# A two-layer graph kernel: its preparation is cut into pieces beside the first node stage, and the target scatters wait for each other in twos

## The chip, the cores and the metric

The kernel runs on one core of a Trainium2 chip. The metric is the device time of one execution in microseconds (us). Engines are called by their names: TensorE (PE in the profile), VectorE (DVE), ScalarE (ACT), GpSimd (POOL) and SyncE (SP).

## What is computed

Two graph layers over 50,000 nodes of 256 float32 features. The edges are 25,000 random ones and a loop at every node, 75,000 in all, sorted by target. Cut to what matters:

```python
h = relu(layernorm(x))
# layer 1: x = x + gcn(batchnorm_mlp(h))
h = h @ w1.T + b1
h = relu((h - mean) * rsqrt(var + eps) * gamma + beta)   # mean, var over all nodes
xw = (h @ w2.T + b2) @ w_gcn.T
deg = segment_sum(ones, dst);  dinv = rsqrt(max(deg, 1))
x = x + segment_sum(xw[src] * (dinv[src] * dinv[dst])[:, None], dst) + b_gcn
# layer 2: edge softmax with 8 heads
h = relu(layernorm(x))
q, k, v = (h @ Wq + bq) * s, h @ Wk + bk, h @ Wv + bv
a = softmax over the edges of one src of (q[src] . k[dst])
x = x + segment_sum(a * v[dst], src) @ Wo + bo
```

## The kernel before

Nodes are handled in 98 tiles of 512 (128 partitions, 4 rows each), two tiles to a pair. Every engine has a program of its own, synchronised by semaphores, and every stage is a block with a barrier at its end. The helper `over_tiles` writes an engine's step for each tile, software-pipelined: TensorE's product of a tile stands three steps behind VectorE's statistics of it, ScalarE's copy of the product four, VectorE's statistics of the copy five. What stands in one step of an engine is executed in the order in which it is written, so the order of the program is that of the code.

**Preparation** (L388 to L691, a block of its own). SP loads the edges (L419) and all weights (L426, 18 loads). POOL writes constants. TensorE turns and mixes weights (L486 and on: `w_mix` is w2 and w_gcn multiplied), ScalarE copies the results from PSUM (L512 to L515). VectorE packs every edge that is no loop and sits in 128 partitions into a word (L530 to L555). Then `takes` rounds (L579 to L584, 15 here) take the 16 largest words of each partition into `found`. The next lines decode the words (from L595), rank them among those of a like target (L629, a scan; L659, a look-up) and give for each of 240 columns the address at which it goes into a table by target (`dst_goal`). VectorE also prepares the attention weights: the peak of `w_qkv` (L649), its scale, its split in two float16 parts (L691), and the three bfloat16 parts of the bias `bo` (L669). Twenty-three semaphores are cleared behind the block.

**First node stage** (L745 to L957). Per tile: SP loads x (L772); VectorE takes row statistics (`row_moments`, L180 and L184); ScalarE takes the square root (`a_std`, L824), VectorE the scales (L191, L193), ScalarE normalises (`a_hn`, L828); TensorE transposes (L853); ScalarE copies (`a_ht`, L818); TensorE multiplies with w1 (L862, eight matmuls into the one PSUM tile `a_h_ps`); ScalarE adds the bias (`h`, L810) and stores the tile (L803); VectorE takes its batch statistics (L918). The same stage counts how many edges end at every node. For each column of 128 edges VectorE makes two one-hot matrices (`hot_hi` L896, `hot_lo` L897) and TensorE adds their product into a histogram in PSUM (L845): five columns a pair, three in the even tile and two in the odd one, over 48 pairs. POOL scatters the same columns to the table by target in memory (L792, 240 indirect DMAs of 128 words), five a pair, paced by `hn_ready` of the pair's tiles. No scatter waits for another; POOL waits for all of them at the end. A loop for edges beyond the regular ones (`count_all`, TensorE from L870, VectorE from L921) runs at the stage's start, once here.

**Second node stage** (L959 to L1362). Batch norm and relu, then the product with `w_mix` (ScalarE L1097, TensorE L1130), per tile; SP loads h1 back (L1052); VectorE adds the bias (L1209) and sorts the edges by source beside it, in 16 bodies of 6 tiles (L1216 to L1252), POOL scatters them (L1343). SP also stores `root_rows` (L1071) and loads `slots` (L1072) at its start. Two later stages do the aggregation with q, k, v and the attention; neither the change nor the prediction touches them.

## Time and profile before

| | us |
|---|---|
| median of 3 runs (3463.72 to 3470.78) | 3466.94 |
| the profiled execution, device time | 3457.55 |
| its span | 3455.8 |
| preparation, from the start to the first table load of the first node stage | 103.4 |
| first node stage, to the end of `dinv` | 637.1 |
| busy over the span: PE | 3100.2 (90%) |
| DVE | 2819.2 (82%) |
| ACT | 2502.9 (72%) |
| POOL | 1945.9 (56%) |

Busy time is an engine's sum over all its instructions; matmuls overlap with weight loads (PEld). A row of the timeline gives the start, the busy time, the engine, the line, output and input, and in brackets how long the engine was idle before and what released it. The granted clock (PEclk) is TensorE's clock as a share of full speed.

### The profile page before, as it was taken

The numbers are of one execution on the slowest core, as the hardware profiler recorded it, in microseconds if no ns is written. First come the engines' busy times: TensorE is split into PE (matmuls) and PEld (weight loads), VectorE is DVE, ScalarE is ACT, GpSimd is POOL, SyncE is SP. The second block draws the span as 40 slices with busy tenths as digits, with TensorE's granted clock in tenths as the row PEclk, the third lists the DMA queues.
The fourth block names the chain that finished last, engine by engine and source line by source line (L and its number), as shares of the span: only waits on it lengthen the run. The fifth ranks groups of instructions, "written<-read, shape, count | busy, mean of one in ns | idle before, by whom it ended". The sixth has DMA issues, their size and how long they took to land. (4 is left out here: it accounts for less than half of the span.)

```text
span 3455.8 us, 80789 instructions
## 1 busy us (share of the span) xinstructions
PE 3100.2 (90%) x20244; PEld 2496.9 (72%) x20244; DVE 2819.2 (82%) x7373; ACT 2502.9 (72%) x7074; POOL 1945.9 (56%) x1668
## 2 busy tenths in 40 slices
PE   1699999799998489999999999994999999999999
PEld 0355555577776368888888888883899999999998
DVE  8788888677787468888888888884888888888887
ACT  0588888689896757777777777762777777777776
POOL 0344444055555277777777777763555555555553
PEclk6799999999999879999999999997999999999999
DMA  1455555488886768888888888875677777777774
GB/s 34 136 201 204 203 201 203 181 301 301 301 307 227 260 233 302 298 307 299 299 302 303 300 297 302 301 273 183 212 256 258 251 253 256 255 251 256 257 250 156
DMA packets 335630, 861.22 MB, mean 249 GB/s; under 512 B 98484, under 2 KB 152923, under 8 KB 323019
## 3 DMA queue, kind: packets, MB, share of 16 engines
q1 hardware_dynamic: 241082, 678.75, 55.2%
q0 software_dynamic: 66256, 78.94, 7.9%
q10 hardware_dynamic: 28224, 102.77, 7.4%
q8 instruction: 25, 0.41, 0.1%
q14 instruction: 43, 0.34, 0.0%
HBM read 521.95 MB, written 416.52 MB: 272 GB/s over the span
## 5 line engine op out<-in xcount | busy, mean ns | idle before, releaser
L1703 PE MATMUL c_qkv_ps<-w_qkv_hi,c_ht_hi 128*128 128x256 f16 x2352 | 642.0, 273 | 0.0
L1703 PE MATMUL c_qkv_ps<-w_qkv_lo,c_ht_hi 128*128 128x256 f16 x2352 | 642.0, 273 | 0.0
L1703 PE MATMUL c_qkv_ps<-w_qkv_hi,c_ht_lo 128*128 128x256 f16 x2352 | 641.9, 273 | 0.0
L2136 ACT ACTIVATE e_mine<-e_mine,e_attention 128x32 f32<-128x32 f32 x2352 | 518.7, 308 | 45.3 <-DVE e_attention L2370 24.3
L2083 POOL DMA_INDIRECT e_kv<-kv_table,e_near x392 | 401.4, 1024 | 113.5 <-issue 102.5
L1573 POOL DMA_INDIRECT c_got<-y_table,c_near x392 | 394.9, 1007 | 109.1 <-issue 90.2
L2172 PE MATMUL e_out_ps<-w_out,e_mean_t 128*128 128x256 f32 x1568 | 392.8, 380 | 0.0
L792 POOL DMA_INDIRECT dst_slots<-dst_word,dst_goal x240 | 236.8, 987 | 267.5 <-ACT a_hn L828 189.2
L2075 POOL TENSOR_TENSOR e_kv<-e_kv,e_part_of 128x1024 f32<-128x1024 f32 x98 | 187.0, 1908 | 350.4 <-DVE e_part_of L2405 350.4
L862 PE MATMUL a_h_ps<-a_ht,w_t 128*128 128x512 f32 x784 | 360.8, 603 | 25.1 <-ACT h L810 21.1
L1343 POOL DMA_INDIRECT src_slots<-staged_word,staged_goal x240 | 233.0, 971 | 260.1 <-DVE sort_lane_hot L1230 129.0
L1130 PE MATMUL mix_ps<-w_mix,hb 128*128 128x256 f32 x1568 | 357.5, 382 | 10.8 <-ACT hb L1097 7.5
L1130 PEld LDWEIGHTS mix_ps<-w_mix,hb 128*128 128x128 f32 x1568 | 296.7, 191 | 57.0 <-ACT hb L1097 10.3
L1566 POOL TENSOR_TENSOR c_x<-c_agg,c_x 128x1024 f32<-128x1024 f32 x98 | 231.3, 2360 | 154.5 <-ACT c_agg L1620 145.5
L2172 PEld LDWEIGHTS e_out_ps<-w_out,e_mean_t 128*128 128x128 f32 x1568 | 267.4, 191 | 44.0
L1690 PE MATMUL c_sum_ps<-c_got,c_sum_hot 128*128 128x256 f32 x784 | 219.0, 403 | 84.0 <-DVE c_agg L1812 48.1
L862 PEld LDWEIGHTS a_h_ps<-a_ht,w_t 128*128 128x128 f32 x784 | 141.4, 190 | 187.8 <-issue 187.8
L1631 ACT ACTIVATE c_hn<-c_x,c_shift,c_rstd 128x256 f32<-128x256 f32 x392 | 203.5, 589 | 95.6 <-DVE c_shift L1833 93.9
L1558 POOL TENSOR_TENSOR c_qk<-c_q,c_kv 128x1024 f32<-128x1024 f32 x98 | 232.0, 2368 | 34.8 <-DVE c_kv L1797 32.6
L1703 PEld LDWEIGHTS c_qkv_ps<-w_qkv_lo,c_ht_hi 128*128 128x128 f16 x2352 | 230.5, 98 | 27.0
L1703 PEld LDWEIGHTS c_qkv_ps<-w_qkv_hi,c_ht_lo 128*128 128x128 f16 x2352 | 230.5, 98 | 26.9
L1703 PEld LDWEIGHTS c_qkv_ps<-w_qkv_hi,c_ht_hi 128*128 128x128 f16 x2352 | 230.5, 98 | 24.7
(432 smaller groups left out, 7683.8 us busy)
## 6 DMA issues: line engine op xcount, KB each, us to landing
kv_table<-c_kv SPq DMA_DIRECT2D x98, 1024.0 KB
h_table<-h ACTq DMA_DIRECT2D x98, 512.0 KB
h<-h_table SPq DMA_DIRECT2D x98, 512.0 KB
y_table<-y_out ACTq DMA_DIRECT2D x98, 512.0 KB
agg_table<-agg_out SPq DMA_DIRECT2D x98, 512.0 KB
c_agg<-agg_table SPq DMA_DIRECT2D x98, 512.0 KB
x_table<-c_x SPq DMA_DIRECT2D x98, 512.0 KB
q_table<-c_q SPq DMA_DIRECT2D x98, 512.0 KB
```

Source lines behind the costliest of these rows:

```text
L792: nc.gpsimd.indirect_dma_start(out=dst_slots, out_offset=bass.IndirectOffsetOnAxis(ap=dst_goal[:, k:k + 1], axis=0), in_=dst_word[:, k:k + ...
L862: last = nc.tensor.matmul(h1_ps[:, oc * TILE:(oc + 1) * TILE], w1_t[:, kc, oc * P:(oc + 1) * P], ht[u][:, kc, :], start=kc == 0, stop=kc = ...
L1130: last = nc.tensor.matmul(mix_ps[u][:, j * D:(j + 1) * D], hb[u][:, kc, j * P:(j + 1) * P], w_mix[:, kc, :], start=kc == 0, stop=kc == KC - 1)
L1343: nc.gpsimd.indirect_dma_start(out=src_slots, out_offset=bass.IndirectOffsetOnAxis(ap=staged_goal[h][:, k:k + 1], axis=0), in_=staged_word ...
L1558: nc.gpsimd.tensor_tensor(qk[u][:, :, :], qb[w][:, :, :], kv[w][:, :, 0, :], ALU.mult).then_inc(qk_ready, 1)
L1566: nc.gpsimd.tensor_tensor(x1[u][:, :, :], agg[w][:, :, :], xb[w][:, :, :], ALU.add).then_inc(x1_ready, 1)
L1573: nc.gpsimd.indirect_dma_start(out=got[w][:, j, :], out_offset=None, in_=y_table, in_offset=bass.IndirectOffsetOnAxis(ap=near[w][:, j:j + ...
L1690: last = nc.tensor.matmul(sum_ps[:, j * D:(j + 1) * D], sum_hot[w][:, row, :], got[w][:, row, :], start=True, stop=True)
L1703: last = nc.tensor.matmul(qkv_ps[n][:, j * D:(j + 1) * D], h[u][:, kc, j * P:(j + 1) * P], wt[:, kc, n * D:(n + 1) * D], start=m == 0, sto ...
L2083: nc.gpsimd.indirect_dma_start(out=kv[w][:, j, :], out_offset=None, in_=kv_table, in_offset=bass.IndirectOffsetOnAxis(ap=near[w][:, j:j + ...
L2136: last = nc.scalar.activation(of_head, of_head, ACT.Copy, scale=attention[u][:, j, h, 0:1])
L2172: last = nc.tensor.matmul(out_ps[:, j, :], mean_t[u][:, kc, row * P:(row + 1) * P], w_out[:, kc, :], start=False, stop=kc == KC - 1)
```

## The change

The preparation's block goes. Its work is split in five:

- **Weights for the first stage.** ScalarE issues seven loads (w1, w2, w_gcn, b1, gamma, beta, b2), TensorE turns and mixes them at the head of its program in the stage, ScalarE copies, and then issues the eight loads of w_out, all before its first tile.
- **Edges.** SP loads them behind the x tiles 0 and 1. VectorE's work on them is cut in pieces, each at the end of its step for one tile (`beside_tile`): tile 1 `pack_words`, tile 3 `close_words`, tiles 4 to 19 one take each, tile 20 the remaining takes (at least one more, so that the rounds are 17 here), 21 to 23 decoding, 24 and 25 marks, 26 the scan, 28 counting, 31 the look-up, 32 to 34 the check, the ranks and the targets, 36 the rest. TensorE's few matmuls for them stand in its steps 30 and 35.
- **Histogram and target scatters** have their columns only from pair 19 (tile 38) on: nine a pair, five in the even tile and four in the odd one, in pairs 19 to 45 (26 x 9 + 6 = 240). The scatters start at the same pair's waits.
- **Scatters in twos.** From the third on, each scatter waits until the one two before it has landed (`dst_put[k % 2]`).
- **The attention weights** are loaded at the start of the second node stage, seven loads in SP's queue ahead of the h1 loads of tile 2 and on. VectorE's `find_peak` stands in the first body of six tiles, `split_weights` in the last one, which is now peeled off the loop. POOL clears 60 semaphores of the first stage and reduces the peak between its first two turns of scatters and its loop.

`count_all` now stands before the last tile's product instead of at the stage's start. The core of the diff:

```diff
+        self.take_pair = 2
+        self.take_pairs = 8
+        self.takes_beside = 2 * self.take_pairs
+        self.class_tile = 2 * (self.take_pair + self.take_pairs)
+        self.hist_pair = self.class_tile // 2 + 9
+        self.hist_most = -(-self.wide // (self.tiles // 2 - 2 - self.hist_pair))
+        self.hist_full = self.wide // self.hist_most
+        self.degree_step = self.tiles + 2
...
-            dst_put = pool_dma_sem("dst_put")
+            ahead = 2
+            dst_put = [pool_dma_sem(f"dst_put{r}") for r in range(ahead)]
...
                     for k in range(WIDTH):
                         pair, c = divmod(k, per_pair)
-                        if c == 0 and pair > 0:
+                        pair += plan.hist_pair
+                        if c == 0:
                             pool.wait_ge(hn_ready[0], pair)
                         if c == per_tile:
                             pool.wait_ge(hn_ready[1], pair + 1)
+                        if k >= ahead:
+                            pool.wait_ge(dst_put[k % ahead], 16 * (k // ahead))
                         nc.gpsimd.indirect_dma_start(out=dst_slots, ...
...
+                    for o, w in ((w1_n, w1), (w2_n, w2), (wg_n, w_gcn)):
+                        act.dma_start(o[:, :, :], halves(w)).then_inc(weights_loaded, 16)
...
+                    for h in range(H):
+                        kc, first = divmod(h * DH, P)
+                        act.dma_start(w_out[first:first + DH, kc, :], rows_of_head[h]).then_inc(out_loaded, 16)
...
+                    def take(n):
+
+                        half = COLS // 2
+                        for h in two:
+                            hold(dve, replaced, n * 2 + (h + 1))
+                            v.max(out=best[h][:, :], in_=words[:, h * half:(h + 1) * half]).then_inc(best_ready, 1)
+                        for h in two:
+                            hold(dve, best_ready, n * 2 + (h + 1))
...
+                        if at(0) is not None:
+                            i, u = at(0)
+                            if k == 0:
+                                take(i * 2 + (u - 2 * plan.take_pair))
+                            elif k is None:
+                                beside_tile(i * 2 + u)
+                        if s == plan.degree_step:
+                            count_all()
...
+                    for i, (w, b) in enumerate(((wq, bq), (wk, bk), (wv, bv))):
+                        sp.dma_start(w_qkv[:, :, i * D:(i + 1) * D], w.rearrange("(c p) n -> p c n", p=P)).then_inc(qkv_loaded, 16)
+                        sp.dma_start(b_raw[:, i * D:(i + 1) * D], b.partition_broadcast(P)).then_inc(qkv_loaded, 16)
+                    sp.dma_start(b_out_n[:, :], bo.partition_broadcast(P)).then_inc(qkv_loaded, 16)
                     over_tiles(sp, plan, 4, step)
...
+                            if isinstance(b, int) and b == 0 and t == 3:
+                                find_peak()
+                            if isinstance(b, int) and b == plan.bodies - 1:
+                                split_weights(t)
...
+                    for s in of_first:
+                        pool.sem_clear(s)
+                    pool.wait_ge(w_peak_ready, 1)
+                    pool.partition_all_reduce(w_peaks[:, :], w_peak[:, :], P, bass.bass_isa.ReduceOp.max).then_inc(w_peaks_ready, 1)
```

Three places in the order of the instructions. The first is VectorE in a tile of the first node stage that carries columns. Before, an odd tile has two of them:

```order
L184 BN_AGGR a_moments<-a_stats 128x2 x3
L896 TENSOR_SCALAR hot_hi<-lane,dst_key 128x392 [waits hot_used1]
L897 TENSOR_SCALAR hot_lo<-lane,dst_lane 128x128
L896 TENSOR_SCALAR hot_hi<-lane,dst_key 128x392
L897 TENSOR_SCALAR hot_lo<-lane,dst_lane 128x128
L191 RECIPROCAL a_rstd<-a_std 128x4 [waits a_std_ready1]
```

Now, from tile 38 on, an odd tile has four:

```order
L221 BN_AGGR a_moments<-a_stats 128x2 x3
L761 TENSOR_SCALAR hot_hi<-lane,dst_key 128x392 [waits hot_used1]
L762 TENSOR_SCALAR hot_lo<-lane,dst_lane 128x128
L761 TENSOR_SCALAR hot_hi<-lane,dst_key 128x392
L762 TENSOR_SCALAR hot_lo<-lane,dst_lane 128x128
L761 TENSOR_SCALAR hot_hi<-lane,dst_key 128x392
L762 TENSOR_SCALAR hot_lo<-lane,dst_lane 128x128
L761 TENSOR_SCALAR hot_hi<-lane,dst_key 128x392
L762 TENSOR_SCALAR hot_lo<-lane,dst_lane 128x128
L228 RECIPROCAL a_rstd<-a_std 128x4 [waits a_std_ready1]
```

The columns stand between the moments, which release ScalarE's square root, and the reciprocal, which waits for it. The second place is VectorE in tiles 4 to 19, the end of a tile's step with a take behind the batch statistics:

```order
L1033 BN_STATS bn_stats<-h_0 128x6
L343 ISA
L839 MAX edge_best<-words 128x8 [waits edge_replaced]
L343 REGISTER_ALU
L839 MAX edge_best<-words 128x8 [waits edge_replaced]
L843 ISA [waits edge_best_ready]
L843 COPY found<-edge_best 128x8
L844 MATCH_REPLACE words<-edge_best,words 128x294
L843 ISA [waits edge_best_ready]
L843 COPY found<-edge_best 128x8
L844 MATCH_REPLACE words<-edge_best,words 128x294
```

The next tile's row statistics stand behind this. The third is POOL, the scatters (`dst_word` to the table `dst_slots`). Before:

```order
L792 DMA dst_slots<-dst_word,dst_goal 50176x1 [waits tables_zeroed]
L792 DMA dst_slots<-dst_word,dst_goal 50176x1 x2
L792 DMA dst_slots<-dst_word,dst_goal 50176x1 [waits a_hn_ready1]
L792 DMA dst_slots<-dst_word,dst_goal 50176x1
L792 DMA dst_slots<-dst_word,dst_goal 50176x1 [waits a_hn_ready0]
```

Now:

```order
L594 DMA dst_slots<-dst_word,dst_goal 50176x1 [waits a_hn_ready0,dst_goals_ready,tables_zeroed]
L594 DMA dst_slots<-dst_word,dst_goal 50176x1
L594 DMA dst_slots<-dst_word,dst_goal 50176x1 [waits dst_put0]
L594 DMA dst_slots<-dst_word,dst_goal 50176x1 [waits dst_put1]
L594 DMA dst_slots<-dst_word,dst_goal 50176x1 [waits dst_put0]
L594 DMA dst_slots<-dst_word,dst_goal 50176x1 [waits dst_put1,a_hn_ready1]
```

Every scatter but the first two has a wait for the one two before it.

## Rows read from the trace of the kernel before

**Rows 1.** Windows: stretch; busy of PE, PEld, DVE, ACT, POOL; PEclk, DMA share, GB/s.

```profile
0.00:103.40 103.40, 11.27 (x33) 7.68 (x33) 86.67 (x275) 3.35 (x5) 8.02 (x37) 0.64 0.11 29
133.60:608.00 474.40, 453.57 (x1691) 239.21 (x1690) 406.31 (x1550) 411.35 (x823) 222.86 (x226) 1.00 0.58 202
638.70:1185.00 546.30, 481.05 (x2297) 367.90 (x2297) 407.19 (x1431) 460.75 (x982) 242.78 (x300) 0.97 0.81 283
```

**Rows 2.** Timeline, the head: start, busy us, engine, line, operation, [idle before <-releaser].

```profile
6.66 3.68 SPq L426 DMA_DIRECT2D w_out<-in_L_gnn_Wo  x8
17.92 1.12 PE L486 MATMUL prep_ps<-ident,w_n 128*128 128x128 f32 x4 [17.92 <-DMA b_c<-in_L_gnn_b]
26.59 0.38 ACT L515 ACTIVATE b_mix<-prep_ps 128x256 f32<-128x256 f32 x1
...
111.56 0.30 ACT L824 ACTIVATE a_std<-a_moments,eps_col 128x4 f32<-128x4 f32 x1 [6.86 <-DVE a_moments L184]
...
128.16 1.40 DVE L180 BATCH_NORM_STATS2 a_stats<-a_x 128x6 f32<-128x256 f32 x4 [2.33 <-DMA a_x<-in_x]
```

**Rows 3.** Timeline, VectorE's pieces of the preparation.

```profile
8.03 0.77 DVE L530 CAST edges_f<-edges 128x1176 f32<-128x1176 int32 x1 [8.03 <-POOL far_end L471]
...
23.98 0.83 DVE L579 MAX8 edge_best<-words 128x8 f32<-128x294 f32 x2 [1.29 <-DVEq L573]
...
25.73 0.83 DVE L579 MAX8 edge_best<-words 128x8 f32<-128x294 f32 x2
...
50.78 0.58 DVE L595 TENSOR_SCALAR src_word<-found 128x816 int32<-128x816 int32 x1 [0.57 <-DVE words L584]
...
63.84 4.50 DVE L629 TENSOR_TENSOR_SCAN up_to<-pair_f,in_class 128x240 f32<-128x240 f32 x8
...
73.36 0.16 DVE L640 TENSOR_SCALAR irregular<-same_ps 128x1 f32<-128x1 f32 x1 [2.74 <-PE same_ps L504]
...
76.53 1.75 DVE L649 TENSOR_REDUCE w_peak<-w_power 128x1 f32<-128x1536 f32 x1
...
90.49 0.28 DVE L669 CAST b_thirds<-b_out_n 128x256 bf16<-128x256 f32 x1
```

**Rows 4.** A pair with columns, a tile without (windows), and a product (timeline).

```profile
402.21:412.59 10.38, 9.92 (x37) 5.24 (x38) 8.97 (x36) 9.00 (x19) 4.94 (x6) 1.00 0.60 202
609.60:614.72 5.12, 4.68 (x16) 2.29 (x17) 3.22 (x12) 4.50 (x10) 1.13 (x2) 1.00 0.39 154
...
614.72 3.67 PE L862 MATMUL a_h_ps<-a_ht,w_t 128*128 128x512 f32 x8 [0.44 <-ACT h L810]
```

**Rows 5.** The stage's first tiles: window, and a product in it (timeline).

```profile
103.40:133.60 30.20, 18.24 (x59) 9.89 (x60) 18.88 (x92) 14.89 (x30) 14.98 (x17) 0.59 0.41 128
...
126.08 4.28 PE L862 MATMUL a_h_ps<-a_ht,w_t 128*128 128x512 f32 x7
```

**Rows 6.** hot_hi: group by line, tile view (ns min/median/max), and two in the timeline.

```profile
L896 DVE TENSOR_SCALAR hot_hi<-lane,dst_key 128x392 f16<-128x392 f16 x193 | 71.3, 370 | 0.0
...
L896 DVE TENSOR_SCALAR hot_hi<-lane,dst_key x193: 306/322/599, 204.3 to 599.6; 128x392 f16<-128x392 f16 x193
...
111.81 0.32 DVE L896 TENSOR_SCALAR hot_hi<-lane,dst_key 128x392 f16<-128x392 f16 x1
...
112.20 0.41 DVE L896 TENSOR_SCALAR hot_hi<-lane,dst_key 128x392 f16<-128x392 f16 x1
```

**Rows 7.** Timeline, two scatters of a pair.

```profile
401.26 0.97 POOL L792 DMA_INDIRECT dst_slots<-dst_word,dst_goal  x1 [4.23 <-ACT a_hn L828]
...
402.53 1.05 POOL L792 DMA_INDIRECT dst_slots<-dst_word,dst_goal  x1 [0.30 <-issue]
```

**Rows 8.** DMA view: queue q0 in 403.2:403.8 (packets); issues elsewhere, us to landing.

```profile
q0 software_dynamic: 32, 0.00, 3.9%
...
state_table<-slow_row_new,slow_goal POOLq DMA_INDIRECT x1, 2.2
...
sum_got<-y_table,sum_from_i POOLq DMA_INDIRECT x1, 4.2
```

More of the change, by code:

```diff
@@ L116, in over_tiles, with over_pairs, turn, at @@
         turn(i, True)
+def over_pairs(eng, plan, lag, step, loops):
+    turns = plan.tiles // 2
+    def turn(i, k):
+        for u in range(2):
+            def at(l):
+                back, slot = divmod(u - l, 2)
+                if k is None and not 0 <= i + back < turns:
+                    return None
+                return i + back, slot
+            step(at, k, i * 2 + u if k is None else None)
+    done = 0
+    for k, (first, last) in enumerate(loops):
+        for i in range(done, first):
+            turn(i, None)
+        with eng.Fori(first, last) as i:
+            turn(i, k)
+        done = last
+    for i in range(done, (plan.tiles - 1 + lag) // 2 + 1):
+        turn(i, None)
 def over_ring(eng, tiles, lead, lag, step):
@@ new lines, in build @@
+            wg_t = sb("wg_t", [P, KC, D], where=prep)
+            b2_c = sb("b2_c", [P, KC], where=prep)
+            work_i = sb("work_i", [P, 2, COLS], I32, where=prep)
+            edges_f = sb("edges_f", [P, 2, COLS], where=prep)
+            apart = sb("apart", [P, COLS], where=prep)
+            same = sb("same", [P, COLS], where=prep)
+            node_of = sb("node_of", [P, COLS], where=prep)
+            ones = sb("ones", [P, COLS], where=prep)
+            same_up = sb("same_up", [P, COLS], where=prep)
@@ new lines, in build @@
+            most = sb("most", [P, 1], where=prep)
+            rounds_f = sb("rounds_f", [P, 4], where=prep)
+            pads_ready = sem("pads_ready")
+            edges_loaded = sem("edges_loaded")
+            const_ready = sem("const_ready")
+            raising = sem("prep_raising")
+            mixed = sem("weights_mixed")
+            chain = sem("prep_chain")
+            counted = sem("edges_counted")
+            most_ready = sem("most_ready")
+            vchain = sem("prep_vector_chain")
@@ L778, in _ @@
+                    for k in range(1, SLOTS, 2):
+                        pool.memset(far_end[:, k:k + 1], float((P - 1) * plan.subtiles)).then_inc(const_ready, 1)
+                    pool.wait_ge(counted, 1)
+                    pool.partition_all_reduce(most[:, :], half_most[:, :], P, bass.bass_isa.ReduceOp.max).then_inc(most_ready, 1)
                     pool.memset(zero[:, :], 0.0).then_inc(zero_ready, 1)
@@ new lines, in _ @@
+                    for o, w in ((w1_n, w1), (w2_n, w2), (wg_n, w_gcn)):
+                        act.dma_start(o[:, :, :], halves(w)).then_inc(weights_loaded, 16)
+                    with nc.allow_non_contiguous_dma(reason="a few hundred words, once"):
+                        for i, b in enumerate((b1, gamma, beta)):
+                            act.dma_start(bn_in[:, i, :], column(b)).then_inc(weights_loaded, 16)
+                        act.dma_start(b2_c[:, :], column(b2)).then_inc(weights_loaded, 16)
@@ L901, in step @@
+                    def step(at, k, s):
                         if at(0) is not None:
```

865 lines of the change are left out of this document (452 added, 413 removed).

## The prediction

> **What bounds the kernel now.** I read the windows by stage first. The preparation stands alone in front: in the first 103.40 us VectorE is busy 86.67 and TensorE 11.27 [rows 1]. The first node stage behind it is bound by no single engine: over a steady 474.40 us TensorE is busy 453.57, ScalarE 411.35 and VectorE 406.31. Then I read the timeline and two windows for the pace of a tile. A product follows the last by 5.12 us where tiles carry no histogram, and starts when ScalarE has freed the one h1 PSUM tile ("<-ACT h") [rows 4]. With five histogram columns a pair takes 10.38. VectorE has room only in tiles without columns (3.22 busy of 5.12), hardly any in the others (8.97 of 10.38, the rest being gaps between dependent instructions). That room is what the change spends.
>
> **The change, part by part.** The sum is made against the profiled execution, 3457.55 us. The median of the runs is 3466.94, 9.4 above, and the sum is carried over to it.
>
> *Head.* Before, the first a_std comes at 111.56 [rows 2]. After, ScalarE issues seven weight loads, then the chain of turning and mixing runs that took from 17.92 to 26.97 before (9.05 us), then ScalarE issues the eight w_out loads (3.68), loads a table and takes the first moments, for which I allow 1.3. The chain waited for b_c, one of 18 loads in one queue, to 17.92; for seven loads, first in theirs, I take half, 9. 9 + 9.05 + 3.7 + 1.3 = 23.0 instead of 111.56: **-88.5** (-93 if the issue is hidden, -82 if the weights land at 15).
>
> *Packing* (tiles 1 and 3) is the stretch 8.03 to 22.69 [rows 3], 14.6 us on VectorE, with the next tile's moments queued behind it. The pipeline is only filling, so two tiles' room (1.5 each) and two waits for x that it covers (2.33 [rows 2], and one like it before) are taken off: 14.6 - 3 - 4.1, **+7.5** (4 to 12).
>
> *Sixteen takes* in tiles 4 to 19: one is 25.73 - 23.98 = 1.75 us. 3.22 + 1.75 and 0.38 allowed for its waits are 5.35, against 5.19 a tile now: 16 x 0.16, **+3** (0 to 8).
>
> *Thirteen pieces* in tiles 20 to 36. From 50.78 to 90.49 are 39.7 us; without the wait of 2.74 for TensorE and without w_peak (1.75) and the pass over the same words ahead of it (some 0.9) they are 34.3, and one take more with its loop is some 3.5: 38. A tile hides at most 5.12 - 3.22 = 1.9, I take 1.6; thirteen hide 21 if all are long enough. Some are short and leave room unused, and the scan (4.50) sticks out whole: **+19** (15 to 26).
>
> *Clock.* At the stage's start, at a granted clock of 0.59 over the stretch, seven of a product's eight matmuls take 4.28; all eight take 3.67 in the steady stage [rows 4, 5]. Behind a piece of 4 to 7 us TensorE stands idle for some us and may fall again. For four such pieces with a tile or two at the lower level, 1 to 2 us each: **+6** (0 to 12).
>
> *Tiles that lose their columns* and have nothing that sticks out are paced at 5.12 instead of 5.19: some 24 of them, **-2**.
>
> *Nine columns in each of 27 pairs.* A column costs VectorE 0.39 from one hot_hi to the next undisturbed (111.81 to 112.20); hot_hi's mean of 370 ns against its least of 306 says what a scatter beside it adds, and hot_lo suffers alike, so 0.50 where scatters fill most of the time [rows 6]. A pair is 2 x 3.22 + 9 x 0.50 + 0.35 of waits = 11.3, against 10.38: 26.67 x 0.92 = **+24.5** (10 to 35). The low end is TensorE's bound, 2 x 5.12 and 0.05 for each column, 10.7. VectorE becomes the bound here; what is late next is a_std, then hn, then the transposes behind it.
>
> *Scatters.* The same 240; nothing else is queued behind them on POOL in this stage but its end, which waits for them. The first five go with tile 36's hn at about 245, the rest from about 260. The pitch is 1.27 now (401.26 to 402.53, 0.97 busy and 0.30 issue) [rows 7]. With a wait for the last but one I take 1.35, so the last goes at 260 + 235 x 1.35 = 577 and has landed by 580. The tiles end at 637 (the end now) - 30.5 (the terms so far) = 606. So **0**, while the pitch stays under (606 - 3 - 260) / 235 = 1.46.
>
> *Degree count* before the last product instead of at the start, where it was part of the head: one turn of its loop, with hand-overs between engines, partly under tiles in flight. **+1.5** (0 to 5).
>
> *Second stage.* Seven loads of together 1.3 MB stand ahead of the third tile's h1 load in SP's queue; at the 283 GB/s of this stage [rows 1] that is 4.6, nearly all seen, since the mix waits: **+4**. find_peak (those two passes, 2.7 [rows 3]) in a body where the sort fills VectorE: **+2**. The splitting in the last body, behind the sort: **+1**. The 60 semaphore clears on POOL before its take loop hide behind the sort: 0 (at most 4). Together **+7** (1 to 14).
>
> Sum: -88.5 + 7.5 + 3 + 19 + 6 - 2 + 24.5 + 1.5 + 7 = **-22**: 3435.5 for the profiled execution, **3445** on the median.
>
> **What speaks against it.** The first scatter of a pair starts at 401.26, and all its 32 packets have moved by 403.8, 2.5 us later. A lone indirect write elsewhere lands after 2.2, a gather after 4.2 [rows 8]. With two under way the pitch is at least half a landing, 1.25 for 2.5. The Trainium skill (DMA: Bandwidth & Descriptors, Anatomy of one DMA — SWDGE (gpsimd) path) states a fixed cost of about 2.0 us a transfer, nearly all of it the receipt of the write; by that and the 0.97 of issue the estimate is 1.5 a scatter and a sum of -14. The trace shows packets but no receipts, and so excludes neither.
>
> **Rivals.**
> - *Scatters a little late.* A landing of 3.0 paces them at 1.5: 260 + 352 + 3 = 615, 8 behind the tiles, **3453**. For it: what comes after the last packet adds to the 2.5. Against: the lone write's 2.2. Chance 0.18. By the page named above this is the case.
> - *Scatters bound the stage* (slower). Under the stage's own traffic, 202 GB/s, a landing of 3.6 makes the pitch 1.8 and the end 260 + 423 + 3 = 686, 49 behind the 637 of now; with the second stage's 7 that is **3523**. At the gather's 4.2 the pitch is 2.1 and the time some 70 more. It shows from a landing of 2.9 and eats the whole gain at 3.1. Chance 0.10.
> - *VectorE lighter than counted.* Columns at 0.44 and pairs of 10.8, near TensorE's bound: 13 less, and 2 less in the pieces, **3430**. For it: the undisturbed 0.39. Chance 0.18.
> - *Clock down through the pieces.* TensorE at 1.2 GHz in eleven tiles, 3.5 to 4 us each, some 44 instead of 6: **3483**. For it: a gap in nearly every tile from 20 to 36. Against: a good half of each tile is still matmuls. Chance 0.08.
> - *Columns and scatters block each other.* POOL is busy 4.94 of a pair's 10.38 now [rows 4], and 9 x 0.98 of 11.3 then. Did each scatter hold a column for half of its 0.97, it would be 240 x 0.5 = 120 instead of 24: **3541**. Against: the longest hot_hi is 599 ns, the median 322 [rows 6]. Chance 0.04. The Trainium skill (SBUF — State Buffer, Who interferes with whom) has VectorE's two-port modes and GpSimd shut each other out for a whole instruction; the trace's 0.1 a column does not agree with it.
>
> **How the numbers follow.** The forecast has 0.42, the rivals the rest. Its own range is 3432 to 3458, from the bounds of the pairs and the pieces. The low end of 3415 has the head, the pairs and the second stage all at their good ends by half; the high end of 3483 takes in the clock. What lies outside is the 0.14 of the two dear rivals and a few hundredths below. A measurement of this kernel tells 0.2%, 7 us, from no change. Faster: forecast 0.42, light 0.18, late scatters 0.13 of their 0.18, together 0.73. Within: 0.09, from late scatters and the clock. Slower: 0.18.
>
> **What would show it.** First a_std at 23; the takes' end, tile 19, near 135; from tile 38 pairs of 11.3 us with VectorE busy over 0.85 of them; scatters 1.35 apart that end before dinv; the stage's end near 607; the third tile's hb 4 us later in the second stage. The forecast is wrong if scatters stand more than 1.46 apart and hold the end of the stage, if the granted clock between tiles 20 and 36 is under 0.8, or if a pair keeps its 10.4.

## The result and the profile after

| | before | after |
|---|---|---|
| median of the runs, us | 3466.84 (3463.72 to 3470.78) | 3525.85 (3519.74 to 3529.64) |
| span of the profiled execution | 3455.8 | 3524.7 |
| first a_std | 111.56 | 25.75 |
| last a_std of the first node stage | 615.4 | 582.7 |
| degree count done (dinv) | 637.13 | 604.37 |
| first h load of the second stage | 638.67 | 697.06 |
| c_slots load, near that stage's end | 1186.0 | 1249.9 |

The change makes the kernel slower: 1.0168 of before, with an interval of 1.0150 to 1.0186. The forecast was 3445, its range 3415 to 3483. The first node stage's own work ends 32.8 us earlier than before, and the second stage starts 58.4 us later.

First the head in the timeline of the kernel after (start, busy us, engine, line, operation, idle before and its releaser), and the same of tile 4:

```profile
11.55 1.12 PE L734 MATMUL a_turn_ps<-ident,w_n 128*128 128x128 f32 x4 [11.55 <-DMA b_c<-in_L_gnn_b]
...
25.75 0.30 ACT L651 ACTIVATE a_std<-a_moments,eps_col 128x4 f32<-128x4 f32 x1
...
52.16 0.30 ACT L651 ACTIVATE a_std<-a_moments,eps_col 128x4 f32<-128x4 f32 x1 [2.59 <-DVE a_moments L221]
```

The head is gone as the diff promised. Then the windows of the stretch with the pieces, of the tiles with columns, and of what lies behind them (columns as in [rows 1]):

```profile
144.00:259.00 115.00, 93.14 (x301) 46.25 (x300) 95.79 (x343) 80.63 (x163) 4.02 (x4) 0.93 0.45 163
...
260.00:560.00 300.00, 293.15 (x1112) 149.45 (x1111) 275.87 (x1125) 239.62 (x491) 150.65 (x153) 1.00 0.55 191
...
604.00:697.00 93.00, 0.00 (x0) 0.00 (x0) 0.37 (x1) 0.00 (x0) 57.27 (x59) 0.50 0.02 3
```

The last row is the loss: for 93 us TensorE and ScalarE do nothing, and the DMA engines move 3 GB/s. Only POOL works. The tile view of its scatters (least, median and longest ns, first and last start), and what ended POOL's idle time before them (us, times):

```profile
L594 POOL DMA_INDIRECT dst_slots<-dst_word,dst_goal x240: 964/971/1203, 251.3 to 693.0; - x120
...
  ACT a_hn L655: 222.7, 3
...
  issue: 100.5, 174
  DMA dst_slots<-dst_word,dst_goal: 99.3, 63
```

A scatter is as short as before, but the first starts at 251.3 and the last at 693.0. The wait for hn is 222.7 us in three pieces, 215 of them ahead of the first scatter; afterwards the pair's hn holds a scatter twice. What holds them is the landing of an earlier one: 63 waits of 1.6 us on average are put down to it. Of the 174 pieces under "issue", 91 are POOL's own 0.30 between two scatters; the other 83, 72.7 us together, are longer, and in front of most of them the wait for `dst_put` is the only one. The timeline shows them in a pair, beside the tiles and behind them, and what waited for the last one:

```profile
443.01 0.96 POOL L594 DMA_INDIRECT dst_slots<-dst_word,dst_goal  x1 [1.39 <-DMA dst_slots<-dst_word,dst_goal]
444.28 0.97 POOL L594 DMA_INDIRECT dst_slots<-dst_word,dst_goal  x1 [0.30 <-issue]
446.31 0.97 POOL L594 DMA_INDIRECT dst_slots<-dst_word,dst_goal  x1 [1.06 <-issue]
448.60 0.97 POOL L594 DMA_INDIRECT dst_slots<-dst_word,dst_goal  x1 [1.33 <-DMA dst_slots<-dst_word,dst_goal]
...
603.80 0.57 DVE L1049 TENSOR_TENSOR dinv<-dinv,a_all_degree 128x392 f32<-128x392 f32 x1
...
639.90 0.97 POOL L594 DMA_INDIRECT dst_slots<-dst_word,dst_goal  x1 [0.66 <-issue]
641.17 0.97 POOL L594 DMA_INDIRECT dst_slots<-dst_word,dst_goal  x1 [0.30 <-issue]
642.85 0.97 POOL L594 DMA_INDIRECT dst_slots<-dst_word,dst_goal  x1 [0.71 <-issue]
...
693.04 0.97 POOL L594 DMA_INDIRECT dst_slots<-dst_word,dst_goal  x1 [0.72 <-issue]
697.06 0.81 SPq L1160 DMA_DIRECT2D h<-h_table  x2
```

Between 260 and 604 a scatter follows the one two before it by 3.83 us on average, a pitch of 1.914. Behind the tiles it is 3.05, a pitch of 1.52 (639.90 to 642.85 is 2.95). Before, a burst went at 1.27 [rows 7].

Last the second stage, its third tile and its end:

```profile
719.21 1.52 ACT L1209 ACTIVATE hb<-h,bn_shift,bn_scale 128x512 f32<-128x512 f32 x2 [10.69 <-DMA h<-h_table]
...
L1649 SPq DMA_DIRECT2D c_slots<-src_slots x1: 338/338/338, 1249.9 to 1249.9; - x1
```

From the first h load to the c_slots load are 552.8 us, against 547.3 before (1186.0 less 638.67), 5.5 more. The loads in SP's queue show in the row (the third tile's hb waits 10.69 us for a load); how the rest of the 5.5 divides was not measured.

### The profile page after: what moved, and what is told of

It reads as the page before. It is cut to its first block and busy times, and to the rows that moved or that the text cites. A ratio compares the mean times of both kernels' runs of the same rounds, so it can differ in the third digit from the quotient of the medians.

```text
span 3524.7 us, 80504 instructions
## 1 busy us (share of the span) xinstructions
PE 3112.4 (88%) x20244; PEld 2493.4 (71%) x20244; DVE 2808.6 (80%) x7391; ACT 2496.1 (71%) x7074; POOL 1948.3 (55%) x1668
## 5 line engine op out<-in xcount | busy, mean ns | idle before, releaser
L594 POOL DMA_INDIRECT dst_slots<-dst_word,dst_goal x240 | 235.4, 981 | 422.5 <-ACT a_hn L655 222.7
L705 PE MATMUL a_h_ps<-a_ht,w_t 128*128 128x512 f32 x784 | 367.9, 613 | 17.9 <-ACT h L637 10.3
L1493 POOL DMA_INDIRECT src_slots<-staged_word,staged_goal x240 | 235.2, 980 | 256.6 <-DVE sort_lane_hot L1382 111.3
L1242 PEld LDWEIGHTS mix_ps<-w_mix,hb 128*128 128x128 f32 x1568 | 297.1, 191 | 59.7 <-ACT hb L1209 11.3
L655 ACT ACTIVATE a_hn<-a_x,a_shift,a_rstd 128x256 f32<-128x256 f32 x392 | 203.3, 589 | 77.8 <-DVE a_shift L230 66.4
```

The source lines that it names most:

```text
L594: nc.gpsimd.indirect_dma_start(out=dst_slots, out_offset=bass.IndirectOffsetOnAxis(ap=dst_goal[:, k:k + 1], axis=0), in_=dst_word[:, k:k + ...
L705: last = nc.tensor.matmul(h1_ps[:, oc * TILE:(oc + 1) * TILE], w1_t[:, kc, oc * P:(oc + 1) * P], ht[u][:, kc, :], start=kc == 0, stop=kc = ...
L1242: last = nc.tensor.matmul(mix_ps[u][:, j * D:(j + 1) * D], hb[u][:, kc, j * P:(j + 1) * P], w_mix[:, kc, :], start=kc == 0, stop=kc == KC - 1)
L1493: nc.gpsimd.indirect_dma_start(out=src_slots, out_offset=bass.IndirectOffsetOnAxis(ap=staged_goal[h][:, k:k + 1], axis=0), in_=staged_word ...
```

## Experiments

The experiments ran on five chips, each time with the kernel before on the same chip. The chips are of two sorts. On three of them the kernel before takes 3455, 3467 and 3465, near the 3467 of the comparison above; I call these A1, A2 and A3. On two it takes 3416 and 3415: B1 and B2. Which sort the comparison above ran on is told by this time alone. That matters further down, so each experiment names its chip, and ratios go only against the kernel before on the same chip.

**1. Three under way** (chip A1, before 3454.62).

```diff
-            ahead = 2
+            ahead = 3
```

> The changed kernel with three scatters under way instead of two. Theory T, that the wait for the landing sets the scatters' pitch (a landing divided by the number under way, never under POOL's own 1.27): at 1.84 us a scatter with two the landing is 3.7, so with three 1.27, the last scatter at about 260 + 235 x 1.3 = 565, before the tiles end at 604; the stage's end comes from 697 to about 607 and the time from 3526 to about 3436, faster than before. Rival N, that nine scatters a pair beside the column work are slow in themselves (descriptors or traffic) and the wait costs little: about 3510 to 3526. Rival Q, that the landing grows with the number under way: pitch stays near 1.8, 3520.

Measured: 3583.71, ratio 1.0367 (1.0350 to 1.0385). The scatters went from 249.6 to 714.2, and the last a_std moved from 582.7 to 743.5. What ended POOL's idle time before the scatters:

```profile
  ACT a_hn L655: 354.3, 16
  issue: 78.3, 209
  DMA dst_slots<-dst_word,dst_goal: 9.8, 15
```

The third place did what theory T said of the scatters: the median distance between two is 1.28, and the waits for a landing shrink from 99.3 us to 9.8. The mean of 1.94 over the whole row comes from stops for hn: 213.6 of the 354.3 us lie ahead of the first scatter, as in the changed kernel, and 140.7 are new, in 15 waits. So the pitch is no longer the limit, and rivals N and Q are out. But now the tiles themselves are late, and T did not have that.

**2. No limit** (chip A1).

```diff
-                        if k >= ahead:
-                            pool.wait_ge(dst_put[k % ahead], 16 * (k // ahead))
```

with one semaphore for all 240.

> The changed kernel with no wait between scatters (one semaphore for all, as before the change). T: POOL's own pitch of 1.27 as with three under way, about 3436; a scatter now runs beside most columns, so a pair may take up to 0.3 more than the 11.1 of the changed kernel, 3436 to 3446. N: over 3500. Q: the pitch of issue is 1.27, but the wait at the end of the stage lasts until the queue is empty, near 3520.

Measured: 3606.33, ratio 1.0429 (1.0406 to 1.0452). The last a_std came at 776.9, the last scatter at 743.9. This contradicts the plain view that the limit alone is at fault: without it the tiles themselves get late. Of this kernel the window over the same 300 us, and the waits in it (engine, line, releaser: us in total, times, longest):

```profile
260.00:560.00 300.00, 194.47 (x692) 99.95 (x690) 178.73 (x704) 148.41 (x299) 145.63 (x148) 0.83 0.34 119
...
POOL dst_slots L591 <- ACT a_hn L651: 97.6, 11, 16.6
ACT h L633 <- remote: 89.9, 8, 15.3
PE a_h_ps L701 <- ACT h L633: 87.7, 7, 15.4
```

TensorE is busy 194 us where it was 293. Now ScalarE waits for something that the trace can't name ("remote"), some 11 us each time, and TensorE and POOL wait for ScalarE. One of these stalls in the timeline:

```profile
422.19 3.67 PE L701 MATMUL a_h_ps<-a_ht,w_t 128*128 128x512 f32 x8
...
430.05 0.38 DVE L221 BATCH_NORM_AGGREGATE a_moments<-a_stats 128x2 f32<-128x6 f32 x4 [3.04 <-remote]
...
437.98 0.97 POOL L591 DMA_INDIRECT dst_slots<-dst_word,dst_goal  x1 [0.30 <-issue]
...
441.46 1.26 ACT L633 ACTIVATE h<-a_h_ps,bn_in 128x512 f32<-128x512 f32 x2 [14.57 <-remote]
```

The product that ScalarE needs is done at 425.86. POOL issues 18 scatters without a pause from 415.58 to 437.98, and ScalarE goes on at 441.46. VectorE too waits 3.04 us, for moments of its own. In the kernel this step of ScalarE waits for three things: the product, VectorE's statistics of the tile two before, and the landing of that tile's store. The semaphore updates in the trace tell them apart: the store's last came at 421.50 and VectorE's at 426.22, but the product's only at 441.30, 15.4 us behind the product's end and 0.16 ahead of ScalarE's start. The work is done, and the news of it is late until the burst is over.

**3. The kernel before with two under way** (chip A1): five a pair from the front, as it was, with the change's limit.

```diff
+                        if k >= ahead:
+                            pool.wait_ge(dst_put[k % ahead], put_base[k % ahead] + 16 * (k // ahead))
```

> The kernel before with the limit of two added and nothing else: five scatters a pair of 10.38 us need 5 x 1.84 = 9.2 or less. T: they fit, 3467, the same as before within 0.2%; the limit alone costs nothing, only with nine in a pair of 11.1 (9 x 1.84 = 16.6). Rival L, that a waiting scatter or its semaphore traffic slows the stage as such: slower than 3475.

Measured: 3455.87, ratio 1.0001 (0.9991 to 1.0011). Its scatters go from 111.6 to 611.3, paced by the pairs. At five a pair from the front the limit costs nothing; it takes the late start with nine a pair for it to hold up the stage.

**4. One under way** (chip A1, one execution).

```diff
-            ahead = 2
+            ahead = 1
```

> The changed kernel with one scatter under way. T: the pitch is a whole landing, 3.7 us beside the tiles and 2.9 to 3.1 behind them (from the idle times of the changed kernel's last scatters): 260 to 604 takes 93 of the 235, the other 142 at 3.0 end at about 1030, the time about 3526 + 333 = 3860 (3800 to 3920). N: little change, under 3600.

Measured: 3820.5. Its tile view:

```profile
L594 POOL DMA_INDIRECT dst_slots<-dst_word,dst_goal x240: 967/967/1211, 250.9 to 1002.0; - x120
...
  DMA dst_slots<-dst_word,dst_goal: 501.0, 234
```

The pitch is 3.39 beside the tiles and 2.94 behind them, while the tiles keep their pace (last a_std 579.9). With one under way the trace tells each scatter's landing, the moment at which its semaphore is full. The DMA view gives the count and the median us from start to landing, first for 260:604, then for 610:1000, and the timeline two scatters of the quiet part:

```profile
dst_slots<-dst_word,dst_goal POOLq DMA_INDIRECT x101, 2.3
...
dst_slots<-dst_word,dst_goal POOLq DMA_INDIRECT x133, 2.1
...
887.23 0.97 POOL L594 DMA_INDIRECT dst_slots<-dst_word,dst_goal  x1 [1.89 <-DMA dst_slots<-dst_word,dst_goal]
890.09 0.97 POOL L594 DMA_INDIRECT dst_slots<-dst_word,dst_goal  x1 [1.90 <-DMA dst_slots<-dst_word,dst_goal]
```

So a scatter that waits for its predecessor follows it by two parts. The landing is 2.1 us after the start when nothing else moves, the same as the lone write's 2.2 in [rows 8]; beside the tiles it is 2.6 on average (median 2.3). Then 0.76 us or more pass from the landing until the next scatter starts: 2.10 + 0.76 = 2.86, the distance of the two rows above. The kernel before shows the second part too, where a scatter waits for hn. ScalarE's a_hn

```profile
398.92 1.57 ACT L828 ACTIVATE a_hn<-a_x,a_shift,a_rstd 128x256 f32<-128x256 f32 x3
```

ends at 400.49 and the scatter that it releases starts at 401.26 [rows 7], 0.77 later; over 45 such waits the median is 0.77.

Half of 2.94 is 1.47, close to the 1.52 that two under way gave behind the tiles; 3.39 halves to 1.70 where two gave 1.91. With two under way on chips B (experiments 8 and 10) the same updates give a landing of 2.8 beside the tiles and 1.1 from the landing to the next start, 0.76 at least: when a place comes free, POOL can still be busy with the other scatter.

**5. Without the scatters** (chip B1, before 3416.38). The kernel leaves the 240 scatters out, so the table by target stays empty and it prices only the rest.

```diff
-                        nc.gpsimd.indirect_dma_start(out=dst_slots, ...
```

> The changed kernel with the 240 target scatters left out (the table by target stays zero, so targets of the edges are missing in what follows); columns, pieces and all else stay. It prices everything of the change but the scatters. If the tile side of the sum is right, the tiles end at about 600 instead of 604 (columns undisturbed, 0.39 each, take up to 24 us off: 580 to 604), the next stage's first load comes at 585 to 608 instead of 697, and the time is 90 to 112 below the changed kernel: 59 less 90 to 112 is 31 to 53 under the kernel before of this chip. Rival: the slow tiles have a cause beside the scatters, and the stage still ends behind 638.

Measured: 3382.71, ratio 0.9898 (0.9881 to 0.9914).

```profile
L644 ACT ACTIVATE a_std<-a_moments,eps_col x98: 283/298/317, 25.6 to 574.8; 128x4 f32<-128x4 f32 x98
...
597.59 0.81 SPq L1153 DMA_DIRECT2D h<-h_table  x2
```

The last a_std comes at 574.8, against 582.7 for the changed kernel on a chip of sort A and 582.9 on B2 (experiment 9) with them: 240 scatters cost the tiles and columns some 8 us. The rest of the change gains 1.0% if the scatters keep out of its way.

**6. No limit behind the tiles** (chip B1).

```diff
-                        if k >= ahead:
+                        if ahead <= k < 186:
```

> The changed kernel with the limit of two for the first 186 scatters only, which covers all that run beside tiles; the last 54 have no wait. Theory S (a scatter beside the stage's traffic costs 1.9 us whatever the limit, and without a limit it is the tiles' stores that land late; with no tile left nothing is hurt): 54 at 1.28 instead of 1.56, 15 less, the time 44 over the kernel before instead of 59. Theory Q (the queue itself takes 1.5 a scatter even alone): no gain, since the end of the stage waits for the landings.

Measured: 3471.79, ratio 1.0160 (1.0143 to 1.0177). The last 54 scatters follow by 1.30 instead of 1.52, which is 12 us less for them, and the last starts at 685.3 instead of 693.0 (the changed kernel, on another chip). POOL's own pitch is nearly reached there, and the chain still ends some 80 us behind the tiles, because some 60 scatters are left when the tiles end. That backlog is made beside the tiles.

**7, 8. The kernel before, not paced by hn** (chip B1), without a limit and with two under way.

```diff
-                        if c == 0 and pair > 0:
-                            pool.wait_ge(hn_ready[0], pair)
-                        if c == per_tile:
-                            pool.wait_ge(hn_ready[1], pair + 1)
```

> The kernel before with POOL's waits for hn left out, so the 240 scatters are issued one behind the other from 111 on, with no limit. Columns stay at five a pair. S: the damage is done by many scatters under way, not by nine columns or the pieces; tiles slow down to about 9 us as without limit in the changed kernel while scatters last (240 at 1.3 to 2.0, 310 to 480 us), 34 to 52 tiles lose 4 us: 140 to 200 over the kernel before. Rival C (the nine columns on VectorE and TensorE make the tiles slow): the same as the kernel before.

> The kernel before with POOL's waits for hn left out and the limit of two. S: scatters stand 1.9 us apart and end at about 111 + 240 x 1.92 = 572, before the tiles at 636; tiles keep 10.4 a pair, the same as the kernel before within 0.3%. Rival: two under way all the time already slow the tiles; slower by 10 us or more.

Measured: 3416.60, ratio 1.0000 (0.9990 to 1.0009), scatters from 111.3 to 428.0 at 1.325; and 3416.37, ratio 0.9999 (0.9989 to 1.0009), scatters to 577.6 at 1.950. Here 240 scatters in one stream disturb nothing, which did not fit experiments 1 and 2.

**9. The change, not paced and without a limit** (chip B2, before 3415.35), and **10. not paced, with the limit** (chip B2): the waits for hn ahead of the scatters removed, in 9 the wait for dst_put too.

> The changed kernel with no limit and without POOL's waits for hn: the 240 scatters go one behind the other from the moment the targets stand (about 240). Theory P, formed after the kernel before took 240 unpaced scatters at 1.32 with no harm: it is the stop-and-go of bursts of nine, each let loose by hn and then stopped, that makes stores land late, not the number under way. Then scatters end at about 240 + 240 x 1.32 = 557 and the tiles at 604; the next stage's first load stands at about 607 to 614 instead of 697 and the time is 25 to 40 under the kernel before. Theory C, that nine columns a pair with unlimited scatters beside them slow the tiles: as without limit, 150 over the kernel before while scatters last (some 100 to 150).

> The changed kernel without POOL's waits for hn, the limit of two kept. The scatters start at 240 instead of 251 and stand 1.92 apart beside the tiles (P and C alike: the limit rules), 190 of them by 604, the rest at 1.55: end near 683 instead of 693. 10 us less than the changed kernel, 49 over the kernel before.

Measured: 9 takes 3388.85, ratio 0.9924 (0.9907 to 0.9940); 10 takes 3462.78, ratio 1.0137 (1.0120 to 1.0154), with its scatters at 1.93 beside and 1.52 behind the tiles, to 681.4. Of 9:

```profile
L587 POOL DMA_INDIRECT dst_slots<-dst_word,dst_goal x240: 966/972/1230, 240.5 to 556.4; - x120
...
L643 ACT ACTIVATE a_std<-a_moments,eps_col x98: 283/298/318, 25.4 to 582.9; 128x4 f32<-128x4 f32 x98
```

The two differ in the limit alone, and by 73.9 us. On this chip the limit is the whole loss, and with neither limit nor waits for hn the change gains 0.76%. The changed kernel just as it is was not run on a chip B.

**11. The kernel before, nine a pair** (chip B2), from pair 19 on, without a limit.

```diff
-                        pair, c = divmod(k, per_pair)
+                        pair, c = divmod(k, 9)
+                        pair += 19
```

> The kernel before with five columns a pair as it is, but the scatters paced as in the changed kernel: nine a pair from pair 19 on, five at the even tile's hn and four at the odd one's, no limit. P: stores land late in bursts of nine and the tiles take 8 to 9 us each from tile 38 on, the stage 100 to 150 longer. C: the columns are five a pair as ever, so the time stays within 10 us of the kernel before.

Measured: 3414.61, ratio 1.0000 (0.9990 to 1.0009), scatters from 301.9 to 626.5 at 1.36, or 1.32 without one stop of 10.1 us behind the first five. Nine scatters at 1.3 take 12 us and a pair takes 10.4, so after that stop hn never held POOL again: this was one stream, as in experiment 7, and did not try bursts with stops between them.

At this point two theories stood: that the waits for hn, given stop-and-go bursts, do the harm of experiments 1 and 2, or that the chips differ. What follows ran on chips A.

**12. The change with its hn waits five pairs earlier, no limit** (chip A2, before 3467.43).

```diff
-                            pool.wait_ge(hn_ready[0], pair)
+                            pool.wait_ge(hn_ready[0], pair - 5)
```

> The changed kernel with no limit, POOL's waits for hn kept in the same places but for the tile five pairs earlier, so that they are always satisfied. Theory P (real stops between long bursts do the harm): as after_unpaced, 26 us under the kernel before. Rival W (the waits among the scatters do it, satisfied or not): as no_limit, about 150 over it.

Measured: 3645.26, ratio 1.0509 (1.0489 to 1.0529); last a_std 797.1. The waits were not satisfied as intended: once the tiles were late, hn of five pairs earlier held POOL 14 times, 156.8 us in all. So this run had stops too and does not tell P from W.

**13. The kernel before in bursts of twelve** (chip A2).

```diff
+                        turn, c = divmod(k, 12)
+                        if c == 0:
+                            pool.wait_ge(hn_ready[0], 4 + 2 * turn)
```

> The kernel before with twelve scatters let loose at every second pair's hn from pair 4 on, no limit: bursts of 12 x 1.3 = 15.6 us, then 5 us of stop in each 20.8. P: tiles stall during the bursts as without limit in the changed kernel (there 15 us in each 38.5); 20 bursts, at least 50 us over the kernel before. Rival D (it also takes the nine columns' load on VectorE): the same as the kernel before within 5 us.

Measured: 3652.98, ratio 1.0535 (1.0519 to 1.0551); last a_std 808.7 instead of some 615. Bursts harm the kernel before too, so nothing else of the change is needed for it.

**14. Experiment 9 with its loads spread** (chip A2): the w_out loads in SP's queue, the attention weights in ScalarE's.

> The changed kernel with its scatters unpaced and without limit, the eight w_out loads issued by SP behind the edges instead of by ScalarE ahead of its first tile, and the seven attention loads of the second stage issued by ScalarE, idle there, instead of by SP ahead of the h1 loads. Against after_unpaced (26.5 under the kernel before): the first a_std 25.4 - 3.6 = 21.8, of which 2 to 3.6 reach the stage's end; in the second stage the third tile's hb no longer waits 10.7 but about 5.6, 3 to 5 less. Together 5 to 8: 31 to 35 under the kernel before, ratio 0.990.

Measured: 3715.76, ratio 1.0718 (1.0704 to 1.0733); last a_std 867.6. The scatters are those of experiment 9, not paced and without a limit, which gained on chip B. The first a_std comes at 23.55, 1.8 sooner than in experiment 9, so that part of ScalarE's issue was not hidden.

**15. Experiment 7 again, the same program** (chip A3, before 3464.83).

> The kernel of before_unpaced once more, which cost nothing on a chip whose kernel before takes 3416. Theory K (chips differ: where the kernel before takes 3455 to 3467, many scatters under way make stores and semaphores late; where it takes 3416 they do not): on a chip of the first sort at least 100 over its kernel before, on one of the second sort the same. Theory P (long bursts with stops only): the same on either.

Measured: 3757.20, ratio 1.0842 (1.0826 to 1.0859). The same window of both, first on chip B1 (experiment 7):

```profile
118.00:420.00 302.00, 285.24 (x1060) 151.54 (x1061) 251.25 (x979) 257.07 (x517) 224.77 (x228) 0.99 0.59 197
```

and on chip A3:

```profile
118.00:420.00 302.00, 48.05 (x130) 24.61 (x130) 29.95 (x126) 29.11 (x59) 226.29 (x232) 0.57 0.09 23
...
ACT h L806 <- remote: 178.7, 4, 48.7
DVE hot_hi L892 <- remote: 13.4, 5, 4.3
```

One program, the same 1.3 us between scatters, and on chip A3 the tiles all but stop: TensorE is busy 48 us of 302 instead of 285, and ScalarE waits 178.7 us in four waits. The product's semaphore tells it again. On B1 every one of the 98 updates stands within 0.02 us of its product's end; on A3 those behind the four waits stand 42 to 47 us behind it. The theory of stop-and-go bursts falls, and with it that of the hn waits, since there are neither here. The two executions differ in the chip; whether it is the chip itself or something that goes with it (which core, what its neighbours do) no run separates. Three chips of sort A showed the harm and two of sort B did not.

**16. Edges in front** (chip A3): a part of the change that should pay on either sort of chip. VectorE runs all the edge pieces ahead of its first tile; the scatters go five a pair from the front, without a limit, as before; the weights are prepared beside the tiles, the attention weights in the second stage with loads by ScalarE, and w_out is loaded by SP.

```diff
-        self.hist_pair = self.class_tile // 2 + 9
-        self.hist_most = -(-self.wide // (self.tiles // 2 - 2 - self.hist_pair))
+        self.hist_pair = 0
+        self.hist_most = -(-self.wide // (self.tiles // 2 - 1))
```

> The pieces of the edges run on VectorE ahead of its first tile, as in the kernel before, with columns and scatters five a pair over all pairs and no limit, as there (which is harmless on both sorts of chip); kept of the change are the weights beside it, the attention weights in the second stage (their loads issued by ScalarE, w_out's by SP) and the count at the end. First a_std at about 90 instead of 111.6, everything behind it as in the kernel before: 21 less, then 1.5 for the count and 1.5 for the second stage: 18 under the kernel before on either sort of chip (12 to 22), ratio 0.995. Rival: the second stage takes it back (ratio 0.998 or more).

Measured: 3449.56, ratio **0.9952** (0.9938 to 0.9965): faster than the kernel before, and so than the change with its 1.0168. It was not run on a chip B.

```profile
L646 ACT ACTIVATE a_std<-a_moments,eps_col x98: 283/315/315, 93.8 to 597.5; 128x4 f32<-128x4 f32 x98
...
620.27 0.81 SPq L1122 DMA_DIRECT2D h<-h_table  x2
637.26 1.52 ACT L1171 ACTIVATE hb<-h,bn_shift,bn_scale 128x512 f32<-128x512 f32 x2 [5.51 <-PE mix_ps L1204]
```

Its scatters end at 592.1, before its tiles. The second stage starts 18.4 us earlier than before and then takes 551.8, 4.5 more than before; the third tile's hb waits again for the mix (5.51), no longer for a load (10.69).

## Why the prediction was wrong

What decided was the rival "Scatters bound the stage", which had a chance of 0.10: a landing of 3.6, a pitch of 1.8, an end at 686, a time of 3523. Measured were 3.83 from a scatter to the one two behind it, 1.91, 697 and 3525.85. That the times agree to 3 us is in part luck. The rival's 3.6 was all landing, where the runs show some 2.8 of landing and 1.1 of restart. And it stood 56 us over the kernel before, where the profiled executions differ by 68.9; the 9.4 us between the profiled execution of before and its median make up most of that.

**The step that failed** is the term of the scatters: "With a wait for the last but one I take 1.35", and from it "So **0**". It rested on "With two under way the pitch is at least half a landing, 1.25 for 2.5". Half a landing is not the whole of it: with a wait in front, a scatter starts 0.76 us or more after the landing that it waited for, and this restart comes on top of every landing. The size of a quiet landing was not the fault. Experiment 4 shows 2.1, and the lone write's 2.2 [rows 8] had it right. 2.1 and 0.8 to 0.9 are the 2.94 and 3.05 measured behind the tiles, a pitch of 1.52 with two places. Beside the tiles' traffic the landing grows to some 2.8 and the restart to 1.1 (experiments 8 and 10); in the changed kernel, beside 191 GB/s, the two together were 3.83, a pitch of 1.91. The restart could have been read before the change, from any scatter released by hn (experiment 4). The threshold in the text, 1.46, was a good one, and it lay below even the quiet pitch.

The Trainium skill (DMA: Bandwidth & Descriptors, Anatomy of one DMA — SWDGE (gpsimd) path) states a fixed cost of about 2.0 us, and the prediction's estimate from it was 1.5 a scatter. The quiet landing of 2.1 agrees with the page, but not its make-up: in experiment 4 the last packet has moved 1.7 us after the scatter's start, so only 0.4 of the 2.1 can be the receipt of the write, where the page has nearly all of it. The quiet pitch of 1.52 agrees with the estimate; the loaded pitch of 1.91 does not, and it is the loaded one that counted. So the chance of the slower side was set too low: the pitch was set by a resource (two places) whose hold time was not added up, with 240 uses on one chain, and the margin was 0.1 us a use.

What it cost: the work beside the scatters was done at 604.4 and the second stage started at 697, some 91 us later. On a chip B the limit costs 74 (experiments 9 and 10, with the scatters starting 11 us sooner). On a chip A taking the limit out does not give these 91 back (experiment 2).

The other terms, in the order of the sum:

| term | forecast | measured | from |
|---|---|---|---|
| head | -88.5 | -85.8 | 25.75 less 111.56; weights land at 11.55, not 9 |
| packing | +7.5 | +5.0 | tile 4's a_std 52.16, before 132.94 |
| sixteen takes | +3 | +9.6 | tile 4 to 20: 92.63, before 83.02 |
| pieces, clock, tiles without columns | +19 + 6 - 2 | +21.1 | tile 20 to 38: 114.5, before 93.4 |
| nine columns a pair | +24.5 | +17.3 | tile 38 to 91: 292.4, before 275.1 |
| degree count | +1.5 | 0 | last a_std to dinv's end: 21.72, before 21.71 |
| scatters | 0 | +91 | dinv's end to the first h load: 92.7, before 1.5 |
| second stage | +7 | +5.5 | 552.8, before 547.3 |

Without the scatters' term the forecast adds up to -22, and the measured terms to -27: the end of dinv was told as 606 and came at 604.37. Two of the smaller ones were off by more than a few us. A tile with a take takes 5.79 us instead of 5.35: the 0.38 for its waits was too little. A pair with nine columns takes 11.03 instead of 11.3, halfway to the 10.8 of the rival "VectorE lighter than counted", and VectorE did not become the fuller engine: in the window 260 to 560 it is busy 0.92 and TensorE 0.98. The granted clock between tiles 20 and 38 was 0.93, so the rival of the clock fell. The rival in which columns and scatters shut each other out fell too: all 240 scatters cost the tiles some 8 us (experiment 5), where the rival had them at 120. That is 0.03 a column; the 0.1 that the sum allowed was too much.

The spans differ by 68.9 and the medians by 59.0, because the profiled execution of before lies 9.4 under its median. By the table the sum of the measured terms up to the second stage's end is +64; 5 more lie in the stages behind it (2274.8 against 2269.8), which the change does not touch, and I have no cause for them.

**What is shown and what isn't.** That the limit of two paces the scatters, by landing and restart, is shown by one, two and three places (3.39, 1.91 and a median of 1.28 beside the tiles), by experiment 10 against 9, and by the semaphore updates in the traces. That the limit costs nothing at five a pair from the front is experiment 3. That removing it would have repaired the change is true on chip B (experiment 9), but on a chip A, the sort that the result above looks like, it is worse than the limit (experiment 2, 1.0429). So the limit is no mere mistake there: nine a pair without it do more harm. That on chips A news between engines comes late beside long runs of small indirect writes is shown by the updates (experiments 2 and 15). Why it does was not settled; no row names what holds it.

## What to carry over

A limit on transfers under way is a pitch: the time from a transfer's start to its semaphore, plus the time from that semaphore to the next start, both under the traffic they will run in, divided by the number allowed. Multiply the pitch by the count on the chain before calling the limit free. Look for both parts in the rows you have: a transfer of that engine that some other semaphore released shows the second. If none shows the first, one run with a single transfer under way does, and it is a lower bound (here 1.70 a scatter where two places gave 1.91). When work is moved later to fill a gap, ask which long, slow chain starts behind it: here 86 us gained at the head put the scatters' start from 111 to 251, and a slow stream over the whole stage, harmless at five a pair, had to fit in two thirds of it.

## What was not expected of the hardware

- The same program took 3416.60 on one chip and 3757.20 on another, where the kernel before took 3416.38 and 3464.83. Its 240 small indirect writes stand 1.3 us apart, with nothing to hold them back. On the second chip a result's semaphore update comes 42 to 47 us after the result beside them, and the engines' waits last up to 48.7 us.
- On chips A the time grew with the number of scatters in a row, each kernel taken by itself: the kernel before in twelves 1.0535 and in one stream 1.0842; the changed kernel without limit, in rows of mostly 18, 1.0429 and in one stream 1.0718 (experiment 14, whose loads differ too). At five a pair, or with two under way, all but at most one of the 98 product updates come within 0.2 us.
- A limit of three is no limit there: the mean distance of 1.91 gave way to rows at 1.28, POOL's own, with stops for hn between them, and the tiles became late as without any: the last a_std went from 582.7 to 743.5 (776.9 without).
- From the semaphore that releases it to its start a scatter takes 0.76 us at least, with the landing of another or with ScalarE's hn as releaser. Beside the tiles it follows by 3.39 with one under way, and the one two back by 3.83 with two.
